# Attention between two feed-forward layers: the second half of the next projection and the odd output projection moved to wide key groups, silu 1 ahead of the first HH

## The reference, cut to what matters

```python
x = x + 0.5 * ffn(layernorm(x), w_gate, w_up, w_down)
x = x + attn(layernorm(x), ...)
x = x + 0.5 * ffn(layernorm(x), w_gate, w_up, w_down)

def ffn(x, w_gate, w_up, w_down):        # 128 -> 384 -> 128
    return (silu(x @ wg.T) * (x @ wu.T)) @ wd.T

def attn(x, ...):                        # 4 heads, 2 key/value heads, head dim 32
    h = rmsnorm(x, norm_w)
    q, k, v = h @ Wq, h @ Wk, h @ Wv     # k, v repeated for 4 heads
    q, k = l2norm(q), l2norm(k)
    p = softmax(where(causal, q @ k.T * exp(log_temperature), -inf))
    return x + gate * ((p @ v) @ Wo)
```

## Time and profile before

| | |
|---|---|
| time, median of 3 executions | 459.48 us (459.06 to 459.52) |
| profiled execution | 459.42 us, its span 457.6 us |
| granted TensorE clock | 0.999 of full speed |
| busy: PE, DVE, ACT, POOL | 413.5, 354.2, 382.8, 260.6 us |
| first feed-forward, attention, second feed-forward | to about 103, 103 to 375, 375 to 457.6 us |

### The profile page before, as it was taken

One profiled execution on the slowest core, in us unless ns is written; L12 is line 12 of the kernel. 1 busy time (PEld: TensorE's weight loads), 2 busy tenths in 40 slices (PEclk: granted clock), 3 DMA queues, 4 the chain that ended last, 5 costly groups with the idle time before them and its releaser, 6 DMA issues.

```text
span 457.6 us, 10470 instructions
## 1 busy us (share of the span) xinstructions
PE 413.5 (90%) x3747; PEld 214.1 (47%) x3747; DVE 354.2 (77%) x872; ACT 382.8 (84%) x546; POOL 260.6 (57%) x321
## 2 busy tenths in 40 slices
PE   0779998989998999999999999999999998999995
PEld 0346665663334335335335335345344244767554
DVE  5899997799499789689689689687647937878654
ACT  3799999667968988988988988988977998999961
POOL 5499999973444444444453553541131456998951
PEclk9999999999999999999999999999999999999999
DMA  5586433334026072084072072092070112557462
GB/s 161 127 163 149 65 53 69 70 71 96 20 53 134 1 140 48 1 140 47 0 138 46 0 138 47 1 139 48 1 139 0 24 26 49 136 93 139 93 116 74
DMA packets 119151, 34.94 MB, mean 76 GB/s; under 512 B 101569, under 2 KB 119105, under 8 KB 119105
## 3 DMA queue, kind: packets, MB, share of 16 engines
q1 hardware_dynamic: 117824, 34.02, 38.9%
q10 hardware_dynamic: 1280, 0.33, 0.3%
HBM read 4.98 MB, written 4.19 MB: 20 GB/s over the span
## 4 chain that ended last, share of the span: by engine, by line
PE 51%; issue 14%; ACT 12%; DVE 11%; POOL 7%; DMA 2%; DVEq 0%; SPq 0%; POOLq 0%; ACTq 0%
PE ps L507 11%; PE ps L706 11%; PE ps L687 9%; PE ps L711 9%; ACT XN L458 4%; PE ps L558 3%; PE ps L569 3%; ACT PT L817 3%; PE ps L594 2%; DVE H L327 2%; ACT SG L476 2%; DVE X L1021 2%; PE ps L691 2%; POOL OL L281 2%; DVE AN L1008 1%
## 5 line engine op out<-in xcount | busy, mean ns | idle before, releaser
L817 ACT ACTIVATE PT<-ps,k_exp 128x1024 f32<-128x1024 f32 (+1 forms) x192 | 162.0, 899 | 20.2 <-PE ps L691 14.8
L507 PE MATMUL ps<-XT,WT 128*128 128x512 f16 x384 | 95.0, 386 | 8.6 <-DVE H L327 3.1
L687 PE MATMUL ps<-QKT 128*128 128x512 f16 (+3 forms) x384 | 87.1, 328 | 11.4 <-ACT PT L817 9.3
L706 PE MATMUL ps<-PT,V 128*32 128x512 f32 (+3 forms) x768 | 81.8, 498 | 0.0
L711 PE MATMUL ps<-PT,ones 128*32 128x512 f32 (+3 forms) x768 | 79.6, 486 | 0.0
L433 POOL TENSOR_TENSOR HL<-H,HH 128x1024 f16<-128x1024 f32 x31 | 67.0, 2160 | 7.3 <-ACT HH L482 5.1
L327 DVE SCALAR_TENSOR_TENSOR H<-SG,k_isilu,ps 128x1536 f32<-128x1536 f32 x32 | 58.0, 1811 | 14.9 <-ACT SG L476 5.6
L281 POOL TENSOR_TENSOR OL<-ON,OH 128x512 f16<-128x512 f32 x15 | 18.2, 1216 | 77.4 <-ACT OH L277 77.4
L687 PEld LDWEIGHTS ps<-QKT 128*128 128x128 f16 x384 | 27.8, 97 | 69.2 <-ACT PT L817 60.1
L507 PEld LDWEIGHTS ps<-XT,WT 128*128 128x128 f16 x384 | 34.6, 99 | 54.1 <-issue 14.5
L458 ACT ACTIVATE XN<-X,NB,RS 128x128 f32<-128x128 f32 x128 | 52.4, 482 | 2.7 <-POOL NB L405 2.7
(11 more groups left out here) (139 smaller groups left out, 645.3 us busy)
## 6 DMA issues: line engine op xcount, KB each, us to landing
result<-X SPq DMA_DIRECT2D x15, 256.0 KB, 2.5
X<-in_L_attn_x SPq DMA_DIRECT2D x7, 512.0 KB, 4.5
X<-in_L_attn_x SPq DMA_DIRECT2D x2, 256.0 KB, 4.9
XT<-w_int SPq DMA_TRANSPOSE x32, 3.1
AXT<-AS SPq DMA_TRANSPOSE x16, 2.8
QKT<-ST SPq DMA_TRANSPOSE x16, 5.6
w_int<-in_L_ffn_w_gate SPq DMA_DIRECT2D x1, 192.0 KB, 4.3
w_int<-in_L_ffn_w_up SPq DMA_DIRECT2D x1, 192.0 KB, 4.5
```

The lines of the kernel that those rows point to most:

```text
L507: i = e.matmul(out[:, j, :], WT[:, wp, w * NJ + j, :], XT[k % 2][:, xp, :], start=a == 0, stop=a == len(passes) - 1)
L687: i_ = e.matmul(o, QKT[k % 2][:, i // TPC, NH + hp, i % TPC * P:(i % TPC + 1) * P], QKT[k % 2][:, qc, 2 * hp + h, CH - n:CH], start=True, ...
L706: e.matmul(PVD[HD * h:HD * h + HD, 0, CH - n:CH], V[k % 2][:, i, v0:v0 + HD], PT[g % 2][:, h, 0:n], start=i == 0, stop=done, skip_group_ch ...
L817: e.activation(PT[g % 2][:, 2 * hp:2 * hp + 2, 0:n], SCORES[hp][:, :, 0:n], ACT.Exp, scale=k_exp[:, 0:1]).then_inc(a_exp, 1)
```

## The change

What it does, part by part: `USES` puts the qkv projection of half 1 of the next batch into group 4 (from 1) and the odd output projection into group 5 (from 3); ScalarE's `qkv_out` of that half follows to 4, the stack casts go to 7 and 8 (from 5 and 6), the casts of x to 10 and 11 (from 9 and 10). Batch 0 keeps its projections and stack casts. GpSimd does the even `o_lo` between the two `stack_lo`. VectorE does the even `o_norm` ahead of `stack_hi2` in every batch. In both feed-forward stages silu 1 stands ahead of HH 0 on ScalarE; in the second, HH 0 is made by VectorE, the first up product waits for the copied sums bank by bank, and the last reciprocal, product and split stand later on VectorE. In the first, VectorE does the statistics of chunk 4 between two parts of the weights' copies.

```diff
             def last_h_hi(k, c):
-                if ph and k == NC - 2:
+                if ph and k in (0, NC - 2):
                     e.wait_ge(s_h, c + NC * ph + 1)
                     e.tensor_copy(HH[k % 2][:, :], hidden_16(k)).then_inc(s_hh, 1)
...
             def h_hi(k, c):
-                if ph and k == NC - 2:
+                if ph and k in (0, NC - 2):
                     return
...
-            early = [(normalise, 0), (normalise, 1), (x_hi, 0), (x_hi, 1), (silu, 0)]
+            early = [(normalise, 0), (normalise, 1), (x_hi, 0), (x_hi, 1), (silu, 0), (silu, 1)]
...
-            def products(k, w, out):
+            def products(k, w, out, bank_free=lambda j: None):
                 passes = [(0, 0), (0, 1)] + [(1, 0)] * low
                 for j in range(NJ):
+                    bank_free(j)
...
-                if ph and k == 0:
-                    e.wait_ge(a_pvc, 4 * B)
-                products(k, 1, U).then_inc(s_up, 1)
+
+                def sums_copied(j):
+                    if ph and k == 0 and j:
+                        e.wait_ge(a_pvc, 4 * B - 2 + j)
+                products(k, 1, U, sums_copied).then_inc(s_up, 1)
...
-        USES = {0: [("qkv", 0, 0), ("qkv", 0, 1)], 1: [("qkv", 1, 0), ("qkv", 1, 1)],
-                3: [("wo", 1)], 8: [("rows", 0)], 10: [("wo", 0)], 11: [("rows", 1)]}
-
-        MOVED = {0: [], 1: [], 3: USES[0], 4: USES[1]}
+        USES = {0: [("qkv", 0, 0), ("qkv", 0, 1)], 4: [("qkv", 1, 0), ("qkv", 1, 1)],
+                5: [("wo", 1)], 8: [("rows", 0)], 10: [("wo", 0)], 11: [("rows", 1)]}
+
+        MOVED = {0: [], 3: USES[0], 4: USES[4]}
...
-                        g_ = g - 3 if k == 0 else g
+                        g_ = ({3: 0, 4: 1} if k == 0 else {0: 0, 4: 1}).get(g)
                         if g_ in (0, 1):
                             qkv_out(k + 1, m0 + g_, k, b, g_)
-                        g_ = g - 2 if k == 0 else g
+                        g_ = g - 2
                         if g_ in (5, 6):
                             stack_hi(m0 + (g_ == 6), int(g_ == 6))
-                    if k + 2 < B and g in (9, 10):
-                        x_hi(m0 + 2 + (g == 10), int(g == 10))
+                    if k + 2 < B and g in (10, 11):
+                        x_hi(m0 + 2 + (g == 11), int(g == 11))
...
                 if nxt:
                     stack_lo(m0, 0)
+                o_lo(e, b * 2)
+                if nxt:
                     stack_lo(m0 + 1, 1)
-                o_lo(e, b * 2)
...
-                if k == 0:
-                    o_norm(e, b * 2, True)
+                o_norm(e, b * 2, k == 0)
                 if nxt:
                     stack_hi2(m0, 0)
                     stack_hi2(m0 + 1, 1)
-                if k >= 1:
-                    o_norm(e, b * 2)
...
-            ffn_act(e, 0, None, {13: first(("v_out", 0, 0), ("v_out", 0, 1), ("squares", 0)),
+            ffn_act(e, 0, None, {0: lambda: ffn_act(e, 0, [("silu", 1)]),
+                                 13: first(("v_out", 0, 0), ("v_out", 0, 1), ("squares", 0)),
...
-                ffn_act(e, 1)
+                ffn_act(e, 1, None, {0: lambda: ffn_act(e, 1, [("silu", 1)])})
...
-            def low_parts():
-                for r in range(2, 5):
+            def low_parts(*parts):
+                for r in parts:
...
+            def low_parts_and_hidden():
+                low_parts(3, 4)
                 e.wait_ge(s_wready, 1)
+                ffn_dve(e, 0, [("hidden", 0)])
...
-            ffn_dve(e, 0, None, {-3: low_parts, -2: lambda: ffn_dve(e, 0, [("hidden", 0)]), NC - 1: stage("second")},
+            ffn_dve(e, 0, None, {-3: lambda: low_parts(2), -2: low_parts_and_hidden, NC - 1: stage("second")},
...
             def finish():
                 ffn_dve(e, 1, [("hidden", 0)])
-                last_reciprocal(e, 0)
-                ffn_dve(e, 1, None, {}, {1: lambda: last_reciprocal(e, 1), 2: lambda: last_norm(e),
-                                            3: lambda: last_split(e)})
+
+                def norm_and_split():
+                    last_norm(e)
+                    last_split(e)
+                ffn_dve(e, 1, None, {}, {1: lambda: last_reciprocal(e, 0), 2: lambda: last_reciprocal(e, 1),
+                                         3: norm_and_split})
```

## The result

The changed kernel takes **476.48 us** (median of 4 executions) against 459.43 us for the kernel before beside it: ratio 1.038, 95% interval 1.035 to 1.041. The forecast was 473.4 us. The four executions are 474.89, 475.04, 477.91 and 479.10 us, with granted clocks of 1.0, 1.0, 0.996 and 0.990; the profiled one is the slowest (span 477.3 us).

A forecast was written before the change was run, and what follows sets the result against it. TensorE, busy 90% of the span, and ScalarE, 84%, were taken as nearly full, with the stacks' transpose room deciding. 459.42 - 0.5 (first feed-forward) - 1.1 (second) + 15.6 (six attention batches) = 473.4 us; range 464.0 to 478.5.

The forecast's parts named there:

- The ring: Attention, first score matmul of one batch to the next: 36.6 us against 34.0, +2.6 for each of six batches.
- The DMA wait: Sign in attention: TensorE's score matmuls wait for the stacks' transpose in every batch, 1.5 to 2.5 us each.
- The waits for OL: Sign in attention: TensorE's waits for GpSimd's OL before the odd output projection, 0.53 us, should be gone.
- The smaller ring: Attention rival, chance 0.12: ScalarE catches up, squares end near 18 us, each batch loses about 1.1 us; 464.4 us.
- The faster case: Attention rival, chance 0.10: stacks stay hidden if their first transpose is issued before 28.9 us; 451.2 us.
- A second wait: Attention rival, chance 0.07: x transpose late too, or VectorE's chain meets GpSimd; +3.6 us per batch, 479.4 us.
- The shared port: Attention stack copies, costed 0.75 us: 0.50 by the port-lock rule (total 1.5 lower), total 1.3 higher by batch 0.
- The stack casts move to steps 7 and 8, under wide groups: Attention, ScalarE's later stack casts: one of the waits costed at nothing.
- First feed-forward: Silu 1 ahead of HH 0 on ScalarE: -0.5 us, bounds -0.9 and +0.2.
- it gains only its two waits of 0.39 us on ScalarE: First feed-forward: GpSimd saves its waits at 57.17 and 66.33 us, 0.39 us, less 0.1.
- Second feed-forward: Silu 1 starts 1.6 us earlier, H 4 about 0.6 us late: net -1.1 us, bounds -1.7 and 0.
- VectorE's step 3: Second feed-forward: normalisation, cast, difference (0.69 + 0.42 + 1.60), H and residual make 5.3 us in a step of 4.58.

The follow-up runs named there:

- run 12: Kernel before with only ScalarE's casts of x moved to groups 10 and 11 (from 9 and 10): 461.92 us against 459.61.
- run 6: Changed kernel with half 1's projection back in group 1, odd output projection in 3, stack casts in 5 and 6: 463.26 us.
- run 5: Changed kernel with half 1's projection back in group 1 and odd output projection in 3, stack casts still in 7 and 8: 471.54 us.
- run 3: Changed kernel with half 1's projection, V copies and squares back in group 1, odd output projection still in group 5: 477.49 us.
- run 2: Changed kernel with VectorE's even reciprocal and product of batches 1 to 6 moved between the stack copies of half 0 and half 1: 491.24 us.
- run 4: Changed kernel with ScalarE's casts of x back in groups 9 and 10 (from 10 and 11): 472.46 us.
- run 7: Changed kernel with VectorE's addition of the odd output moved from ahead of the products with the norms to behind the stack copies: 475.81 us.
- run 9: Kernel before with only the first feed-forward's part of the change: 459.15 us, ratio 1.0004.
- run 11: Kernel before with the second feed-forward's part, VectorE's last normalisation one step sooner, with the second half reciprocal after H 2: 457.92 us, ratio 0.9977.
- run 1: Kernel before with only the attention part of the change (tables, casts and orders): 475.70 us, ratio 1.037.
- run 10: Kernel before with only the second feed-forward's part of the change: 459.52 us, ratio 1.0014.

## Why the prediction was right, and what it missed

**The rings together.** Times from a batch's first score matmul, in steady batches. A group number of 5 for the stack casts means 5 and 6, and so on.

| kernel | qkv half 1 / odd output / stack casts / x casts in group | squares end | stack cast starts | transpose issued | ring |
|---|---|---|---|---|---|
| before | 1 / 3 / 5 / 9 | 11.98 | 20.68 | 23.52 | 33.98 |
| run 12 | 1 / 3 / 5 / 10 | 12.45 | 21.15 | 24.00 | 34.46 |
| run 6 | 1 / 3 / 5 / 10 | 12.45 | 21.15 | 24.66 | 34.46 |
| run 5 | 1 / 3 / 7 / 10 | 12.44 | 26.90 | 29.75 | 35.52 |
| run 3 | 1 / 5 / 7 / 10 | 12.45 | 27.40 | 30.48 | 36.23 |
| changed | 4 / 5 / 7 / 10 | 19.80 | 27.11 | 30.77 | 36.54 |

(Runs 3, 5, 6 and the changed kernel have the reciprocal ahead of the stacks.) In the last three, issue plus 5.77 us is the ring, to 0.02 us. The issue comes at 29.75 us with the stack cast late, at 30.48 with the odd output later too, at 30.77 with the squares late as well: three limits within 1.0 us of each other. The middle one is not VectorE's addition alone. In run 3 the stack cast itself starts 0.50 us later than in run 5 (27.40 for 26.90), and the copies start at 28.55, 0.3 us after the cast's end, because VectorE's chain behind the addition is not done sooner. The steps from row to row (0.48, 0, 1.06, 0.71, 0.31 us) add up to the 2.56 us, but each says only what its edit costs on top of those above it.

**The ring, term by term: right.** Squares end at 19.8 us (forecast 19.5); sums, norms, addition and products take 6.07 us (232.21 to 238.28; forecast 6.13), reciprocal and product 4.40 (4.33), copies to issue 0.47 (0.85), transfer 5.77. With 0.03 us ahead of the sums that is 36.54 against 36.6. That the two agree to 0.1 us is in part luck: the squares came 0.3 us later and the copies took 0.4 us less than costed. That the transpose becomes late, and that VectorE's chain from the squares ends last, was the mechanism. The DMA wait is 1.4 us and not 1.9 (nor within the 1.5 to 2.5 that were to show it), since TensorE is ready at 35.15 us and not at 34.7: it lost 1.2 us instead of 0.7. The rows above say where. TensorE is ready at 34.46 us with the casts of x late, at 34.61 with the stack casts late too, at 35.10 with the odd output in group 5, and the moved half adds 0.05. The waits for OL are gone as said. TensorE's busy time did not stay at 32.3 (33.07).

**The rivals.** The smaller ring (squares near 18 us) did not come: 19.8. The faster case hung on an issue before 28.9 us; it is 30.77. A second wait, for the transpose of x, came in one batch each of runs 2, 4 and 6 (0.79, 0.45 and 0.64 us), and in none of the changed kernel.

**The shared port.** The stack copies took 0.49 us together, the lower bound, with GpSimd's difference done at 242.21. The Trainium skill, SBUF — State Buffer, "SBUF: two separate sides", calls the port pair that VectorE (in a two-port mode, or with two SBUF inputs) and GpSimd share an exclusive lock, which whoever starts first holds for its whole instruction. By that rule run 7's copy had to grow, and L263 had to take 2.50 us behind HL and 0.69 us ahead of it; the traces agree. But the saved time had been spent one instruction earlier: the product started 0.13 us behind that same difference and ran 1.09 us instead of 0.69.

**"The stack casts move to steps 7 and 8, under wide groups": costed at nothing, and wrong as a step.** Runs 5 and 6 differ in these casts alone: with them in groups 7 and 8 every batch waits for the DMA and the ring is 35.52 us, with them in 5 and 6 none does and it is 34.46. (No run moved them in the kernel before and nothing else.) It did not falsify the total, because the squares' chain ends 1.0 us later than the cast's. A reader who had undone only what the forecast blamed would have gained nothing (run 3).

**First feed-forward: -0.5 forecast, 0 measured.** The failed step is "it gains only its two waits of 0.39 us on ScalarE": in run 9, as in the changed kernel, GpSimd's waits at 57 and 66 us are still there (0.37 and 0.43 us, for 0.39 each before; the first of them in the earlier trace rows). In the changed kernel H 0 came at 22.19 (22.15 forecast) and GpSimd's HL 0 at 26.65, about as costed (26.5).

**Second feed-forward: -1.1 forecast, +0.5 measured.** The early part was right: silu 1 starts 6.12 us after the first gate product instead of 7.90. The failed term is VectorE's step 3. It was costed with the split's 0.42 and 1.60 us; beside GpSimd they took 1.27 and 2.50. That is 1.75 us on top of what was costed. From H 3 to H 4 the changed kernel takes 6.84 us, where 5.3 were costed and the kernel before has 4.57; more than the whole gain went into it. Run 11 takes the same edit with the step thinned, and is 1.1 us faster.

**Attention beyond the rings.** In run 1's profile, six rings give 14.8 us (218.85 against 204.02) where 15.6 were forecast; the last batch gives 0.4 us more (30.75 against 30.37), costed at 0 with bounds -0.3 and +0.7. The medians are higher, 16.8 us for the attention part and 17.0 for the whole, and the likeliest reason is that single transposes come late. The kernel before has them too. The time from issue to landing of its 16 stack transposes, from the view of line L1235:

```profile
DMA to landing us min/median/max: 5.4/5.6/7.4
```

Two of those for a half 0 took 7.2 and 7.4 us (issued at 196.74 and 298.70), but there the matmul came 10.5 us after the issue and nobody waited. The change used up the room that hid them. In the profiled execution of the changed kernel the late one is the last. Stretches (busy times, clock, DMA share, GB/s) and TensorE:

```profile
355.00:360.00 5.00, 1.67 (x29) 1.02 (x22) 0.75 (x1) 0.46 (x2) 0.23 (x1) 0.89 1.24 158
360.00:365.00 5.00, 5.00 (x36) 2.40 (x36) 0.59 (x1) 3.82 (x5) 0.00 (x0) 0.50 0.45 102
...
359.92 1.01 PE L690 MATMUL ps<-QKT 128*128 128x512 f16 x2 [3.33 <-DMA QKT<-ST]
```

Issued at 352.42, it was waited for until 359.92, 7.5 us for the usual 5.77. After the idle 3.33 us TensorE was granted half its clock (0.50, that is 1.2 for 2.4 GHz) from 360 to 365 us, and a pair of wide score matmuls took 1.01 us instead of 0.59. The same stretch of run 1, with a wait of 1.57 us, had a clock of 1.00. The changed kernel's ring of 38.09 us there (36.33 in run 1) and its last batch of 32.66 us (30.75) are together 3.7 us, most of the 4 us by which this execution is longer than those with clock 1.0. So the median carries a part that the forecast did not have. The 3.1 us between the forecast and the median are then, term by term: rings -0.8, last batch +0.4, the feed-forwards +2.1 (+0.5 measured for -1.6), and 1.4 us left over for late transposes and their clock, a remainder and not a measurement.

## What to carry to other kernels

When a stage is moved later, list every producer that its consumer needs (here the squares, the output's addition, the stack cast, the reciprocal) and work out the ready time of each, not only of the one that looks last: an operation "hidden under wide groups" was a limit of its own 1 us behind. The room must also cover the latest transfers, not only the usual one. A short wait of the busiest engine is worth less than the slack that its removal spends; here 1.1 us of waits were traded for an issue 7.3 us later in the ring. On engines that slow each other, try the short instruction just ahead of the long one, and not just behind it (run 11, in one place, together with a normalisation one step sooner: 1.6 us against run 10).

## What the runs showed of the hardware that had not been expected

- VectorE's difference of 512 columns in fp16 took 0.69 us when it started 0.1 us before GpSimd's 1024-column one, and 2.50 us when it started 0.4 us after it; GpSimd's then took 2.57 and 2.31 us. In the kernel before it took 1.60 us, 0.1 us behind a 512-column difference of GpSimd's.
- Transposes of the same 0.79 MB mostly took 5.77 us from issue to the matmul that waited (5.4 to 5.6 us to landing), but single ones 7.2 to 7.4 us to landing, 7.5 to the matmul. Such ones are in every profile but run 2's, that of the kernel before too. TensorE waited longer only where one for a half 0 was late and had no room: the last one in the changed kernel and in runs 3, 5 and 7, and one in the middle of run 3. Why they come late stays open; no run was made on it.
- With each of these five waits, of 2.68 to 3.33 us, the granted clock fell to 0.50 toward its end or soon behind it, and stayed there for 3 to 7 us. In four of them the first matmul already took 0.91 to 1.01 us for 0.59; behind the wait of 2.77 us in run 3 (until 361.35) it took 0.59 us and the clock was at half only from 363 us on. Behind the DMA waits of up to 2.0 us in these profiles it stayed at 1.00. Run 2 has a wait of 2.91 us for ScalarE in every batch: behind four of the six the clock was at half for some 3 us, behind two it was not. Stretches of run 3, and of run 2 behind its first and second such wait (174.57 and 214.17):

```profile
363.00:366.00 3.00, 3.00 (x21) 1.06 (x16) 0.78 (x1) 3.00 (x6) 0.00 (x0) 0.50 0.08 17
...
175.50:178.50 3.00, 3.00 (x29) 1.76 (x29) 2.60 (x9) 1.11 (x2) 1.32 (x3) 0.51 0.39 73
...
215.00:218.00 3.00, 3.00 (x43) 1.77 (x44) 3.00 (x10) 1.60 (x4) 1.32 (x3) 1.00 0.36 70
```
